# Scores of four latent heads in common rounds, and a first hidden chunk whose value and gate share one product

## The reference, cut to what matters

```python
# x: (8, 512, 256)
xn = layernorm(x)
s  = retention(xn)                 # 4 heads, chunks of 64 tokens
g  = silu(local_ffn(xn))           # two layers, below
x  = x + s * g
xn = layernorm(x)
s  = latent_attention(xn)          # 16 heads, below
g  = silu(experts(xn))             # top 2 of 8 experts, F = 1024
x  = x + s * g

def layer(x, ...):                 # of local_ffn, twice
    h = shift_token(x)
    q, k, v = split(h @ wqkv)      # 8 heads of 64
    q, k = rotary_xpos(l2norm(q) * qs, l2norm(k) * ks)
    x = x + local_attention(q, k, v) @ wo        # window 128
    h = layernorm(shift_token(x))
    a, g = split(h @ w1 + b1)      # hidden size 682 each
    return x + (a * gelu(g)) @ w2 + b2

def latent_attention(x):           # keys and queries of 24 per head
    scores = clip(Q @ K.T, -80, 80)
    scores = where(causal, scores, -inf)
    return (softmax(scores / sqrt(24)) @ V) @ W_O
```

## Time and profile before

| | us |
|---|---|
| median of three runs | 2849.97 |
| lowest and highest | 2844.25, 2851.5 |
| the profiled execution's own time | 2849.19 |
| its span | 2847.4 |
| mean granted clock of TensorE | 0.978 |

### The profile page before, as it was taken

The page is one execution under the profiler, slowest core; times in us unless marked ns, Lnnn a source line. Parts: engine busy times, 40 slices in busy tenths (PEclk is TensorE's granted clock), DMA queues, the critical chain, the costliest instruction groups (busy, mean ns, idle before and its releaser), DMA issues.

```text
span 2847.4 us, 41985 instructions
## 1 busy us (share of the span) xinstructions
PE 2703.8 (95%) x15582; PEld 1833.3 (64%) x15582; DVE 1546.2 (54%) x3730; ACT 1235.8 (43%) x2287; POOL 1051.0 (37%) x726
## 2 busy tenths in 40 slices
PE   6999999999999999999999999999997799999993
PEld 4575757566575757555555555555564578999993
DVE  6565566575666555677676767576855322100004
ACT  4454444545453444545454545454543234222222
POOL 5434243443434243445454536363623122111110
PEclk9999999999999999999999999999998899999997
DMA  4000000000001001101010101010000666899987
GB/s 143 12 16 26 26 16 30 27 27 16 26 16 57 18 24 52 61 5 53 4 53 5 53 4 45 12 39 19 30 34 23 235 247 250 304 365 365 360 334 243
DMA packets 85907, 261.83 MB, mean 92 GB/s; under 512 B 10668, under 2 KB 49916, under 8 KB 67020
## 3 DMA queue, kind: packets, MB, share of 16 engines
q1 hardware_dynamic: 75004, 237.19, 23.0%
q0 software_dynamic: 6480, 17.77, 1.7%
q10 hardware_dynamic: 4224, 4.19, 0.4%
HBM read 210.81 MB, written 44.11 MB: 90 GB/s over the span
## 4 chain that ended last, share of the span: by engine, by line
PE 65%; issue 13%; DVE 10%; POOL 6%; ACT 3%; DMA 2%; SPq 0%; POOLq 0%; DVEq 0%; ACTq 0%
PE s_pD L722 19%; PE s_pA L722 18%; PE s_pD L878 5%; PE s_pA L772 3%; PE s_pD L794 3%; PE s_pA L781 3%; PE s_pA L1167 2%; PE s_pD L1182 2%; POOL acc_s L1598 2%; DVE s_qk L1676 2%; POOL s_rinv L1501 2%; PE s_pA L761 1%; DMA s_z<-s_cur 1%; PE s_pA L733 1%; PE s_pA L888 1%
## 5 line engine op out<-in xcount | busy, mean ns | idle before, releaser
L1507 POOL TENSOR_TENSOR s_qk<-s_qk,s_rrec 128x1024 f32<-128x1024 f32 (+1 forms) x128 | 220.7, 1725 | 502.7 <-DVE s_rrec L1682 502.5
L722 PE MATMUL s_pA<-s_w_wqkv,s_curT 128*128 128x512 f32 x768 | 354.6, 602 | 5.6 <-ACT s_curT L1212 3.7
L1236 ACT ACTIVATE s_qk<-s_qk,s_mx 128x256 f32<-128x256 f32 (+1 forms) x512 | 239.8, 471 | 95.3 <-DVE s_mx L1676 95.3
L1775 DVE TENSOR_SCALAR s_pairs<-s_pD 128x1024 f32<-128x1024 f32 (+1 forms) x192 | 195.0, 1040 | 151.4 <-PE s_pD L878 150.1
L722 PEld LDWEIGHTS s_pA<-s_w_wqkv,s_curT 128*128 128x128 f32 x768 | 142.6, 191 | 176.7 <-issue 163.2
L1501 POOL TENSOR_TENSOR s_rinv<-s_ssq,s_half 128x16 f32<-128x16 f32 x64 | 230.1, 3596 | 59.5 <-DVE s_ssq L1661 59.5
L1598 POOL DMA_INDIRECT acc_s<-s_w_w,s_sq x71 | 68.5, 964 | 470.7 <-ACT s_w_w L1444 463.5
L2139 DVE COPY s_w_wo<-s_pD 128x256 f32<-128x256 f32 x71 | 29.9, 421 | 338.5 <-PE s_pD L1153 338.5
L1466 POOL TENSOR_TENSOR s_rs<-s_ve,s_half 128x4 f32<-128x4 f32 x40 | 42.0, 1050 | 433.4 <-DVE s_ve L1636 433.3
L878 PE MATMUL s_pD<-s_mixer 32*128 32x512 f32 (+3 forms) x1024 | 180.7, 467 | 11.9 <-DVE s_pairs L1775 9.0
L722 PE MATMUL s_pA<-s_zT,s_w_w 128*120 128x512 f32 (+1 forms) x384 | 183.8, 601 | 4.2 <-ACT s_pairs L1281 3.1
(11 more groups left out here) (268 smaller groups left out, 5724.6 us busy)
## 6 DMA issues: line engine op xcount, KB each, us to landing
s_qkT<-in_m_w SPq DMA_DIRECT2D x48, 1024.0 KB, 6.7
s_v_tm<-in_m_w SPq DMA_DIRECT2D x24, 1024.0 KB, 7.4
s_rot<-in_m_w SPq DMA_DIRECT2D x24, 1024.0 KB, 6.3
s_w_wqkv<-in_m_w SPq DMA_DIRECT2D x23, 1024.0 KB, 7.7
s_qk<-in_m_w SPq DMA_DIRECT2D x23, 1024.0 KB, 5.7
s_w_w<-rows_s SPq DMA_DIRECT2D x71, 129.0 KB, 6.0
s_cur<-in_x SPq DMA_DIRECT2D x8, 512.0 KB, 3.5
xn_s<-s_cur SPq DMA_DIRECT2D x8, 512.0 KB, 2.6
```

What stands on the lines that cost most here:

```text
L722: last = nc.tensor.matmul(out, lhs(c), rhs(c), start=(c == 0), stop=(c == n - 1))
L1236: last = nc.scalar.activation(pi, pi, ACT.Exp, scale=-1.0, bias=mx[:, u, i:i + 1], accum_out=rsum[:, u, i:i + 1])
L1507: nc.gpsimd.tensor_tensor(pi, pi, rrec[:, u, :].unsqueeze(2).broadcast_to((P, 4, 256 - lo)), ALU.mult).then_inc(p_rdy, 1)
L1775: nc.vector.tensor_scalar(Pl[:, w % SLOTS, :, ROUND_AT[r]:ROUND_AT[r] + ROUND_N[r]], ps[:, :, 0:ROUND_N[r]], 80.0, -80.0, ALU.min, ALU.max ...
```

## The change

First, the **hidden chunks** are cut anew: the first has 42 columns, five have 128 (in sum 682). The value columns of chunk 0 (rows 0 to 41 of the product) and its gate columns (rows 64 to 105, `GATE`) stand in one block of 106 columns of w1, so chunk 0 is a single product on ring D and its g product on ring A is gone. Gelu of chunk 0 reads the bank of ring D and signals `first_gelu`; gate_up of chunk 0 waits for it and sets the row of ones, which now belongs to chunk 0.

Second, of the **rows of zeros** before the experts SyncE writes those of experts 0 to 3; those of experts 4 to 7 are issued by ScalarE in stage 15, at u = 5.

Third, in stages 9 to 14 the **scores** of pairs 4 and 5 are made by `four_scores`, a round of both pairs at a time, on all four row groups. A round of both takes the whole ring D, two jobs of two banks. Round 0 and round 1 stand before and behind the q and k product of t = 0, round 2 ahead of that of t = 1. The clips follow in the same order. Exp and mask of pair 4 move from t = 0 to t = 1, those of pairs 5 and 6 (the mask) to t = 2 and 3.

The diff, cut to its core:

```diff
 HID = 682
-HCH = 120
+HCH = 128
 NHC = 6
-HSZ = [min(HCH, HID - HCH * c) for c in range(NHC)]
+HSZ = [HID - HCH * (NHC - 1)] + [HCH] * (NHC - 1)
+HAT = [0] + [HSZ[0] + HCH * c for c in range(NHC - 1)]
+GATE = 64
+ONES = 32
+UPW = GATE + HSZ[0] + 2 * HCH * (NHC - 1)
 
...
         for c in range(NHC):
-            if s.here:
+            if s.here and c:
                 j += [("g", k, c)]
...
         for t in range(NT):
-            if s.behind and t < 3:
+            if s.behind and (s.last and t < 3 or t == 2):
                 j += pair(b - 1, 4 + t)
+            if s.behind and not s.last and t < 2:
+                j += [("sc", b - 1, 4 + i, r) for r in ((0, 1) if t == 0 else (2,)) for i in range(2)]
             if s.ret:
...
             sp.dma_start(S["rows"][E * REG:E * REG + P, :], zrows).then_inc(zero_in, 16)
-            def zero_rows(e):
+            for e in range(E // 2):
                 n = sp.value_load(counts_i[0:1, e:e + 1], min_val=0, max_val=B * T)
                 sp.dma_start(S["rows"][bass.ds(n + e * REG, P), :], zrows).then_inc(zero_in, 16)
-
-            for e in range(E // 2):
-                zero_rows(e)
 
...
                 if u == 0:
-                    for z in range(E // 2, E):
-                        zero_rows(z)
                     for k in range(TOPK):
...
             def up_projection(b, c):
-                n = HSZ[c]
                 if c == 0:
                     pe.wait_ge(outA, doneA["zT", b, 1])
-                ps = slotA("g", b, c)
-                project(ps[0:n, 0:T], lambda k: W["w1"][:, k, HID + c * HCH:HID + c * HCH + n], lambda k: zT[:, k, :], DC).then_inc(mmA, 1)
+                n = HCH if c else GATE + HSZ[0]
+                at = GATE + HSZ[0] + 2 * HCH * (c - 1) if c else 0
+                if c:
+                    ps = slotA("g", b, c)
+                    project(ps, lambda k: W["w1"][:, k, at + HCH:at + 2 * HCH], lambda k: zT[:, k, :], DC).then_inc(mmA, 1)
                 ps = slotD("a", b, c)
-                project(ps[0:n, 0:T], lambda k: W["w1"][:, k, c * HCH:c * HCH + n], lambda k: zT[:, k, :], DC).then_inc(mmD, 1)
+                project(ps[0:n, 0:T], lambda k: W["w1"][:, k, at:at + n], lambda k: zT[:, k, :], DC).then_inc(mmD, 1)
 
             def down_projection(b, i):
-                rows = [min(HCH, HSZ[c] + (c == NHC - 1)) for c in range(NHC)]
+                rows = [HSZ[c] + (c == 0) for c in range(NHC)]
                 if i == 0:
...
                     last.then_inc(mmD, 1)
+
+            def four_scores(b, g, r):
+                pe.wait_ge(outD, doneD["lq", b, g])
+                ps = [slotD("sc", b, 2 * g + pr, r) for pr in range(2)]
+                last = {}
+                for kt, col in ROUNDS[r]:
+                    for h in range(4):
+                        rows = slice(32 * h, 32 * h + 32)
+                        i = h % 2
+                        last[h] = nc.tensor.matmul(ps[h // 2][:, 512 * i + col:512 * i + col + T - kt * P], KT[rows, g % 2, tile_cols(kt)],
+                                                   QT[rows, g % 2, kt * P:T], start=True, stop=True)
+                last[1].then_inc(mmD, 1)
+                last[3].then_inc(mmD, 1)
 
...
                 for t in range(NT):
-                    if s.behind and t < 3:
+                    if s.behind and (s.last and t < 3 or t == 2):
                         latent_scores(b - 1, 4 + t, (0, 1))
+                    if s.behind and not s.last and t < 2:
+                        four_scores(b - 1, 2, 2 * t)
                     if s.ahead:
...
                         ret_products(k, t)
-                    if s.behind and t < 3:
+                    if s.behind and (s.last and t < 3 or t == 2):
                         latent_scores(b - 1, 4 + t, (2,))
+                    if s.behind and not s.last and t == 0:
+                        four_scores(b - 1, 2, 1)
                     if s.ahead:
...
                 n = HSZ[c]
-                ps = takeA("g", b, c)
+                at = 0 if c else GATE
+                if c:
+                    ps = takeA("g", b, c)
+                else:
+                    act.wait_ge(mmD, DJ["a", b, 0] + 1)
+                    ps = pD[:, colsD[DJ["a", b, 0]]]
                 if b > 0 or c >= 2:
                     act.wait_ge(outD, doneD["a", b, c - 2] if c >= 2 else doneD["a", b - 1, NHC - 1])
-                nc.scalar.activation(gl_of(b)[c % 2][0:n], ps[0:n, 0:T], ACT.Gelu, bias=W["b1"][0:n, 1, c:c + 1]).then_inc(outA, 1)
+                last = nc.scalar.activation(gl_of(b)[c % 2][0:n], ps[at:at + n, 0:T], ACT.Gelu, bias=W["b1"][at:at + n, 1, c:c + 1])
+                last.then_inc(outA if c else first_gelu, 1)
 
...
                         ret_copy("rv", k, t, rv[:, t, :])
-                    if s.behind and t < 2:
+                    if s.last and t < 2:
                         latent_exp(b - 1, 4 + t)
+                    if s.behind and not s.last and t in (1, 2):
+                        latent_exp(b - 1, 3 + t)
                     if s.behind and t == 3 and not s.last:
...
                         values_in(b, 1)
+                    if s.last and u == 5:
+                        act.wait_ge(zero_rdy, 2)
+                        act.wait_ge(weight_rdy, TOPK * LAST + 1)
+                        for e in range(E // 2, E):
+                            n = act.value_load(counts_i[0:1, e:e + 1], min_val=0, max_val=B * T)
+                            act.dma_start(S["rows"][bass.ds(n + e * REG, P), :], zrows).then_inc(zero_in, 16)
                     if s.last and u == 6:
...
                         reciprocal_roots(var_h, rstd_h, k)
-                    if s.behind and t < (2 if s.last else 3):
+                    if s.last and t < 2:
                         causal(b - 1, 4 + t)
+                    if s.behind and not s.last and t:
+                        causal(b - 1, 3 + t)
                     if s.ahead:
...
                 n = HSZ[c]
-                if c == NHC - 1:
-                    step(nc.vector.memset(hT_of(b)[NHC - 1][64:HCH], 1.0))
                 ps = take("a", b, c)
-                dve.wait_ge(outA, doneA["g", b, c])
+                if c:
+                    dve.wait_ge(outA, doneA["g", b, c])
+                else:
+                    dve.wait_ge(first_gelu, b + 1)
+                    step(nc.vector.memset(hT_of(b)[0][ONES:2 * ONES], 1.0))
                 nc.vector.scalar_tensor_tensor(out=hT_of(b)[c][0:n], in0=ps[0:n, 0:T], scalar=W["b1"][0:n, 0, c:c + 1], in1=gl_of(b)[c % 2][0:n],
...
                 for t in range(NT):
-                    if s.behind and t < 3:
+                    if s.behind and (s.last and t < 3 or t == 2):
                         clipped(b - 1, 4 + t, (0, 1))
+                    if s.behind and not s.last and t < 2:
+                        clipped(b - 1, 4, (2 * t,))
+                        clipped(b - 1, 5, (2 * t,))
                     if s.here and t == 0:
...
                         ret_rotary(k, t)
-                    if s.behind and t < 3:
+                    if s.behind and (s.last and t < 3 or t == 2):
                         clipped(b - 1, 4 + t, (2,))
+                    if s.behind and not s.last and t == 0:
+                        clipped(b - 1, 4, (1,))
+                        clipped(b - 1, 5, (1,))
                     if s.past and t == 1:
```

More of the change, by code:

```diff
@@ L2217, in arrange @@
     r["w_ln"] = np.stack([np.stack([per(g), per(b)], 1) for g, b in zip(a["L0_ffn_ln_g"], a["L0_ffn_ln_b"])], 1)
-    r["w_w1"] = np.stack([ch(w) for w in a["L0_ffn_w1"]], 1)
+    up = []
+    for c in range(NHC):
+        value = a["L0_ffn_w1"][:, :, HAT[c]:HAT[c] + HSZ[c]]
+        gate = a["L0_ffn_w1"][:, :, HID + HAT[c]:HID + HAT[c] + HSZ[c]]
+        room = np.zeros(value.shape[:2] + (0 if c else GATE - HSZ[0],), np.float32)
+        up += [value, room, gate]
+    r["w_w1"] = np.stack([ch(w) for w in np.concatenate(up, 2)], 1)
     b1 = np.zeros((HCH, DEPTH, 2, NHC), np.float32)
@@ L2224, in arrange @@
             for i in range(2):
-                b1[0:n, l, i, c] = a["L0_ffn_b1"][l, i * HID + c * HCH:i * HID + c * HCH + n]
-            w2[0:n, l, c] = a["L0_ffn_w2"][l, c * HCH:c * HCH + n]
-        w2[HSZ[-1], l, NHC - 1] = a["L0_ffn_b2"][l]
+                at = 0 if c or not i else GATE
+                b1[at:at + n, l, i, c] = a["L0_ffn_b1"][l, i * HID + HAT[c]:i * HID + HAT[c] + n]
+            w2[0:n, l, c] = a["L0_ffn_w2"][l, HAT[c]:HAT[c] + n]
+        w2[HSZ[0], l, 0] = a["L0_ffn_b2"][l]
     r["w_b1"], r["w_w2"] = b1, w2
```

3 lines of the change are left out of this document (2 added, 1 removed).

## The result

The changed kernel takes 2890.39 us (median of four runs, 2887.86 to 2891.51) against 2850.73 before: a ratio of 1.0141, 95% interval 1.0126 to 1.0155. It is slower, as forecast, but by 40 us where 14 were forecast, and outside the stated range. Later groups of runs had the kernel before at 2845 to 2848; each experiment is compared with the before of its own group.

What follows compares the result with a forecast made beforehand. TensorE was taken to bound the eight retention stages and GpSimd's queue the six long ones; 2849.2 - 13.8 - 1.3 - 1.7 - 3.5 + 6 x 5.8 = 2863.7, about 2864 us, range 2846 to 2884.

Steps and rivals of the forecast that it cites:

- the two waits: Stages k = 9 to 14: TensorE waits 4.4 us for clips ahead of round 2, then 5.0 for the mask before latent_values.
- the prediction's 5.4: Six long stages: upper bound in us of the 4.0 per stage, the delay of latent_values counted in full.
- the first low stretch: Half clock behind the wait for the clips: 6.8 us costing 3.4, of which about 1.2 reaches GpSimd's queue.
- 8 x 1.72 = 13.8 us saved: Eight retention stages: each saves the g product of chunk 0, 1.72 us, in full.
- 5.8 us per stage: Six long stages: cost of the common rounds, 4.0 from GpSimd's chain plus 1.2 and 0.6 from the clock.
- clock terms: Six long stages: half clock adds 1.2 us behind the first wait and 0.6 behind the second.
- The bound of 8.5: Six long stages: upper bound in us per stage, both half-clock stretches twice as long and half uncovered.
- the rows of zeros: Before the experts' phase: ScalarE's earlier issue shortens TensorE's idling, gain 3.5 us, between 2.5 and 4.5.
- no clock loss: Rival for the six long stages: the same delays without a lower clock, 2853 us, chance 0.20.
- four heads not side by side: Rival for the score rounds: a common round costs two, 2868 us, chance 0.06.
- the long loss: Rival for the six long stages: longer clock loss, 8.5 us per stage, 2880 us, chance 0.12.
- The other side: Rival: mask of pair 5 early enough, delays don't reach the stage's end; 2829 down to 2807 us, chance 0.12.

Runs made afterwards that it cites:

- e1: Changed kernel with chunk 0 at full height (128 rows) in the down projection and a second memset ahead of gate_up of chunk 1; 2881.2 us, ratio 1.0120.
- e7: Changed kernel with exponentials and masks of pairs 4 and 5 ahead of rotary_sum(1), clips left as they were; 2868.8 us, ratio 1.0076.
- e8: Changed kernel with round 1 of pairs 4 and 5 clipped ahead of the fourth tile of shifted_stats, masks left late; 2849.8 us, ratio 1.0012.
- e9: Changed kernel with both edits of order, the early masks and the early clips of pairs 4 and 5; 2828.2 us, ratio 0.9936.
- e3: Changed kernel with pairs 4 and 5 back in the order of before on all engines, the common rounds undone; 2845.4 us, ratio 0.9999.
- e11: Changed kernel with pairs 4 and 5 in the order of before and chunk 0 at full height in the down projection; 2837.6 us, ratio 0.9965.
- e4: Kernel before with the common rounds alone, chunks and rows of zeros as before; 2899.1 us, ratio 1.0184.

## Why the prediction was wrong

**Direction and the two waits were right.** Both stand where the prediction put them: 4.40 us for 4.4 ahead of round 2, 3.44 us for 5.0 ahead of latent_values (shorter, since TensorE itself comes there 3.2 us later); the granted clock falls behind both. The four heads run side by side. From the start of latent_values of group 1 that of group 2 comes after 41.1 us (1704.14 to 1745.23) against 34.5 (1684.53 to 1719.00), 6.6 us late, which is the prediction's 5.4 (its delay in full) and the 1.2 that it gave the first low stretch. Its rounding (1720.8 and 3.75 make 1724.55 and not 1724.4; 1724.4, 2.80 and 3.32 make 1730.5 and not 1731) moves nothing here.

The forecast was +14.5 us over the span and the measurement +40.2. Of the 25.7 between them 9.2 lie ahead of stage 8, 13.7 in the six long stages (48.5 for 34.8), and the rest in stage 8 and at the end.

**The step that failed first: the term "8 x 1.72 = 13.8 us saved", with nothing against it for the rest of the chunks.** The a product did stay at 1.72, but the term priced only the product that was taken away and not what the new sizes do in the down projection. There a chunk of 43 rows among chunks of 128 costs TensorE 1.2 us a stage, as e1 showed by giving that back (128.7 to 127.6). The gain up to stage 8 was 4.6 us in place of 13.8, 9.2 of the miss.

**The step that failed second: the term "5.8 us per stage", which hung the stage on the mask and let the first wait be swallowed.** It measured 8.1. The prediction gave the wait for the clips 1.2 us ("the next wait swallows most of it") and the mask 4.0 and 0.6, and said that with the mask early enough the stages keep their length. In e7 the mask is early, latent_values waits for nothing, and a stage is still 4.8 us longer than before; in e8, where the clips are early and the mask late, it is 1.4 longer. So the first wait was the dear one.

The trace shows the path that was missed. The prediction let the 5.4 us at latent_values shrink to 4.0 at the end of the chunk loop, because GpSimd's chain would hide the rest. The trace has the next fixed point, the product behind gelu(3), at 1772.07, 67.9 us after latent_values of group 1, against 60.6 before (1745.17): 7.3 us late, more than at latent_values. GpSimd itself was quicker than forecast: the mask of pair 5 took 3.6 us, near the prediction's busy price, but that of pair 6, behind 7.48 us of an idle VectorE, took the quiet price of 2.6, where the prediction had 3.3. But it did not run on by itself. VectorE's clip of pair 7 waited for TensorE's slow scores, and behind that clip stand rotary_parts and the square sums of the last tile (one row of VectorE, then GpSimd's):

```profile
1751.54 2.36 DVE L1814 TENSOR_SCALAR s_pairs<-s_pD 128x1024 f32<-128x1024 f32 x2 [7.48 <-PE s_pD L882]
```

```profile
1751.70 1.27 POOL L1551 TENSOR_TENSOR s_pairs<-s_pairs,s_tri 128x512 f32<-128x512 f32 x1
1756.44 2.35 POOL L1532 TENSOR_TENSOR s_qk<-s_qk,s_rot 128x1024 f32<-128x1024 f32 x1 [3.46 <-DVE s_qk L1694]
1760.27 3.82 POOL L1536 TENSOR_TENSOR s_rinv<-s_ssq,s_half 128x16 f32<-128x16 f32 x1 [1.49 <-DVE s_ssq L1698]
```

The prediction had rotary_sum(3) run right behind the mask, and 0.5 us of waiting for the square sums; they were 3.46 and 1.49. Head_norms(3) began 56.1 us after latent_values of group 1 where the prediction's times have 52.8; of the 3.4 between them its clock terms cover 1.8. In the stage shown the 7.3 us are all of its growth (146.6 to 153.7); the mean growth of the five is 8.1. The bound of 8.5 held it; the likeliest value did not.

Of the clock, the raw price was near (3.4 us for each stretch, so 6.8 a stage; 5.5 of TensorE's busy time by e9), and the 1.8 of it that the prediction let through to the stage's length was too little.

**Right in size:** the rows of zeros, 2.9 us of idling for 3.5 (too little to be proved alone). Stage 8 was put at -1.3 and is +0.2. **Rivals:** that of no clock loss is out by the windows; four heads not side by side is out by the rows of 1.14 us; the long loss (2880) was nearest, though by another way than it said. The other side was not met by the change. e9, at 2828, comes to the prediction's 2829 partly by luck: it needs the clips early too, its long stages are 1.6 us shorter than before and not level, and its retention stages gain about 0.5 us and not 1.72.

The Trainium skill's page "TensorEngine Tiling (Array Packing)", section "PSUM Bottleneck", pointed the right way: after tiling, the clips set the pace. The trace agrees in that TensorE waits 4.40 us for them. e8 and e9 show that what they cost here was mainly their place in VectorE's queue, and not their duration: two clips take 2.36 us in the changed kernel and in e9, and the wait falls to 1.20 and 1.24 us.

**Why full height gave nothing in k = 9 to 13.** The windows of these five stages of e3 and then e11:

```profile
1232.30:1966.00 733.70, 706.64 (x4062) 418.49 (x4060) 507.99 (x1166) 376.06 (x645) 359.36 (x251) 0.99 0.08 28
1223.30:1956.10 732.80, 700.46 (x4062) 419.45 (x4060) 505.95 (x1171) 375.55 (x645) 355.45 (x251) 0.99 0.08 28
```

TensorE's busy time did fall by 1.2 us a stage (706.64 to 700.46), and its idling rose by 1.0. Of its waits, the one for gelu grew by 0.6 us a stage (2.6 to 5.8 in the five), behind the second memset, and the one of the transposes of the probabilities (L781) by 1.0 (1.5 to 6.3, half of it with no releaser named). So in these stages TensorE's saving turned into waiting.

**What stays open:** why two stages of e4 have a lower clock than its others, from which height between 64 and 83 on a product is free of the cost, and what waits of another length would cost in clock.

## What to carry to other kernels

When work is packed into fewer, larger rounds that need a whole ring of banks, look at what stands ahead of the evacuation on its engine: here two clips moved by one place in VectorE's queue, and two masks by one on GpSimd's, turned a loss of 8 us a stage into a gain of 1.6. When a tile size is changed to save an instruction, follow the new size to every product that reads it, and look whether neighbouring products still have like heights: here 43 or 64 rows beside 128 cost time, 83 beside 120 did not. A wait of TensorE of 3 to 4 us can cost its length and, in the clock behind it, as much again (e7: 3.1 and 3.2 us a stage) or somewhat less (e8: 1.7 and 1.3); a forecast should not let a chain hide that unless the chain itself does not hang on TensorE.

## What the runs showed of the hardware that was not expected

A change of height between products of 43 or 64 rows and of 128 rows came with a gap of 0.33 us ahead of the next weight load and cost some 0.2 us for each change (e1 took both away); 83 beside 120 rows does not. Idle stretches of 3.44 and 4.40 us were followed by 4.8 and 5.7 us at 0.50 and 0.56 of the clock; one of 4.07 us in e8 cost less, 6.0 us at 0.72, with 4.03 us for the latent_values that take 2.36 at full clock.
